# 65 places in the 72-step order of an attention block changed on four engines, and the quantiser's scale computed by GpSimd

## The reference

```python
h = layernorm(x) * (1 + ca) + sa
x = x + ga * attention(h, Wq, Wk, Wv, Wo)     # 32 query heads on 8 key heads of 64, rotary, causal
h = layernorm(x) * (1 + cb) + sb
x = x + gb * ffn(h, w_gate_up, w_proj)
# the ffn's weights are quantised in groups of 64:
#   w = w.astype(bf16); scale = clip(mean(|w|), 1e-8); q = clip(round(w / scale), -1, 1)
#   w + (q * scale - w)
# ffn: silu(gate) * up, rms_norm, projection
```

## Time and profile before

| | us |
|---|---|
| median of 3 runs (lowest, highest) | 1829.48 (1827.33, 1831.39) |
| profiled execution, its own time | 1831.12 |
| its span, first to last instruction | 1829.2 |
| mean granted TensorE clock | 0.990 of full speed |

### The profile page before, as it was taken

The page is one execution under the profiler, slowest core; times in us unless marked ns, Lnnn a source line. Parts: engine busy times, 40 slices in busy tenths (PEclk is TensorE's granted clock), DMA queues, the critical chain, the costliest instruction groups (busy, mean ns, idle before and its releaser), DMA issues. The chain is left out here.

```text
span 1829.2 us, 28097 instructions
## 1 busy us (share of the span) xinstructions
PE 1740.6 (95%) x9505; PEld 1390.7 (76%) x9505; DVE 1249.0 (68%) x2102; ACT 1147.0 (63%) x2315; POOL 968.3 (53%) x773
## 2 busy tenths in 40 slices
PE   7899999999999999999999999988999899999998
PEld 3577777877777777777787787776788788888886
DVE  6788888888787878788888888785333454535343
ACT  4578777777777777877777777795322353323222
POOL 1266757666667676566766666636200044444454
PEclk9899999999999999999999999999999999999999
DMA  7333434344354354344434434455555300101010
GB/s 279 78 103 95 124 103 128 103 108 123 88 132 116 87 129 109 92 120 105 125 104 108 122 89 139 110 162 164 179 180 183 126 1 1 52 1 52 1 30 23
DMA packets 174969, 190.95 MB, mean 104 GB/s; under 512 B 31456, under 2 KB 117736, under 8 KB 174832
## 3 DMA queue, kind: packets, MB, share of 16 engines
q1 hardware_dynamic: 137840, 140.99, 27.1%
q10 hardware_dynamic: 36992, 48.25, 9.5%
HBM read 86.12 MB, written 31.74 MB: 64 GB/s over the span
## 5 line engine op out<-in xcount | busy, mean ns | idle before, releaser
L980 DVE TENSOR_TENSOR p_lo<-ps_b,p_hi 128x512 fp32r<-128x512 f32 x576 | 395.6, 687 | 190.9 <-ACT p_hi L876 187.1
L891 ACT ACTIVATE p<-ps_b,negm 128x640 f32<-128x640 f32 (+7 forms) x512 | 381.8, 749 | 123.2 <-DVE negm L988 120.1
L876 ACT CAST p_hi<-ps_b 128x512 fp32r<-128x512 f32 x576 | 337.2, 588 | 128.1 <-PE ps_b L774 125.5
L988 DVE TENSOR_REDUCE negm<-ps_b 128x1 f32<-128x640 f32 (+7 forms) x512 | 375.7, 744 | 33.3 <-PE ps_b L764 32.5
L774 PE MATMUL ps_b<-ident,p 128*128 128x128 f32 x2304 | 348.7, 274 | 6.2 <-DVE p_lo L980 5.3
L762 PE MATMUL ps_b<-k_hh,q_hl 128*128 128x512 f32 (+3 forms) x768 | 272.7, 355 | 45.5 <-ACT p L891 44.8
L774 PEld LDWEIGHTS ps_b<-ident,p 128*128 128x128 f32 x2304 | 260.3, 141 | 46.7 <-ACT p L891 7.9
L788 PE MATMUL ps_b<-p_hi,v_hl 128*128 128x512 f32 x576 | 269.8, 468 | 5.6 <-ACT o_sb L884 5.2
L763 PE MATMUL ps_b<-k_l,q_hl 128*128 128x512 f32 (+3 forms) x768 | 256.8, 347 | 0.0
L789 PE MATMUL ps_b<-p_lo,v_hl 128*128 128x512 f32 x576 | 227.1, 394 | 0.0
L762 PEld LDWEIGHTS ps_b<-k_hh,q_hl 128*128 128x128 f32 x768 | 145.6, 190 | 94.1 <-ACT p L891 64.8
(11 more groups left out here) (161 smaller groups left out, 3201.8 us busy)
## 6 DMA issues: line engine op xcount, KB each, us to landing
rot_x<-rot_s SPq DMA_DIRECT2D x320, 64.0 KB, 2.0
q_hl<-rot_s SPq DMA_DIRECT2D x128, 128.0 KB, 2.5
q_hl<-rot_x SPq DMA_DIRECT2D x128, 128.0 KB, 2.5
rd_all<-reciprocals SPq DMA_DIRECT2D x128, 128.0 KB, 3.0
o_low<-o_sb ACTq DMA_DIRECT2D x128, 128.0 KB, 2.4
attention_out<-o_sb SPq DMA_DIRECT2D x128, 128.0 KB, 2.5
o_raw<-attention_out SPq DMA_DIRECT2D x32, 512.0 KB, 4.6
wf<-in_L_ffn_w_gate_up ACTq DMA_DIRECT2D x28, 256.0 KB, 3.1
```

The lines of the kernel that those rows point to most:

```text
L876: act.copy(p_hi[:, T % P_RING, :], ps[:, T_BANK + T % 2, :]).then_inc(phi_ready, 1)
L891: act.activation(p_32[:, parity, h, column * P:column * P + nk], s, ACT.Exp, bias=negm[:, k:k + 1], scale=1.0, accum_out=den[:, parity, k: ...
L980: dve.tensor_tensor(p_lo[:, T % P_RING, :], ps[:, T_BANK + T % 2, :], p_hi[:, T % P_RING, :].bitcast(F32), ALU.subtract).then_inc(plo_read ...
L988: dve.tensor_reduce(negm[:, k:k + 1], s, AX.X, ALU.max, negate=True).then_inc(max_ready, 1)
```

## The change

The functions that said in which step a part is due (`rows`, `tile`, `uses`, `pairs`, `units`, `blocks`) are replaced by tables, one for each kind of part, from the part's number to a pair (step, place in the step). Most entries hold the old step and the old order within it. 65 entries are changed ("own" is the old step; a place is a number that sorts the parts within a step). The mask (L764) becomes a part of its own, `masked`, which may stand apart from its row's scores. The scale of a weight unit, 128x8 elements, is computed by GpSimd, in the unit's step 5. `above` is gone: `unit_pick` multiplies by the constant and compares in one scalar_tensor_tensor. `split_weights` is divided in two functions that stand one behind the other in the same step; ScalarE's `unit_parts` is divided likewise.

```diff
+TURNS = Places(own_tiles(0), 100, {
+    11: (10, 303), 19: (18, 511), 20: (19, 511), 25: (24, 511), 35: (34, 511), 39: (38, 301), 66: (65, 101),
+    71: (70, 511)})
+VALUES = Places(own_tiles(LAG), 200, {
+    0: (2, 900), 2: (4, 511), 3: (4, 512), 8: (10, 301), 9: (11, 900), 16: (18, 900), 18: (20, 900), 23: (24, 512),
+    24: (26, 900), 27: (29, 900), 32: (34, 900), 36: (38, 900), 44: (46, 501), 45: (47, 900), 52: (54, 900),
+    54: (56, 900), 55: (58, 101), 60: (62, 900), 63: (65, 900), 68: (70, 900)})
+PROJECTIONS = Places(own_pieces(), 300, {
+    (0, 0): (1, 101), (0, 2): (4, 101), (2, 0): (9, 800), (3, 0): (14, 101), (3, 1): (14, 102), (4, 0): (19, 800),
+    (4, 2): (22, 101), (5, 0): (24, 800), (5, 1): (27, 101), (5, 2): (27, 102), (6, 0): (31, 201), (7, 0): (36, 501),
+    (7, 3): (38, 901), (9, 0): (44, 800), (10, 0): (49, 501), (11, 0): (54, 800), (12, 0): (59, 501), (12, 1): (61, 201),
+    (12, 2): (62, 101), (13, 0): (67, 501), (13, 2): (69, 301)}, early=PROJECTIONS_EARLY)
+VALUE_TURNS = Places(own_uses(("v",), 0), 400, {
+    1: (6, 501), 8: (41, 201)})
+SCORES = Places(own_rows(0), 500, {
+    6: (6, 520), 14: (15, 501), 22: (24, 520), 30: (33, 520), 38: (42, 520), 46: (51, 501), 54: (60, 501), 62: (69, 520)}, early=SCORES_EARLY)
+MASKS = Places(own_rows(0), 510, {
+    6: (6, 530), 8: (10, 302), 14: (15, 530), 22: (24, 530), 30: (33, 530), 38: (42, 530), 46: (51, 530), 54: (60, 530),
+    62: (69, 530)}, early=MASKS_EARLY)
...
+HIGHS = Places(own_tiles(0), 200, {
+    18: (17, 301), 30: (29, 311), 40: (39, 601), 66: (65, 201)})
+SHIFTS = Places(own_blocks(LAG + 1), 310, {
+    13: (67, 401)})
+EXPONENTIALS = Places(own_rows(1), 400, {
+    6: (7, 420), 14: (16, 420), 22: (25, 420), 30: (34, 420), 32: (37, 201), 38: (43, 420), 46: (52, 420), 54: (61, 420),
+    62: (70, 420)}, early=EXPONENTIALS_EARLY)
+KEY_HIGHS = Places(own_uses(("kv",), 8), 500, {
+    13: (76, 201)}, early=in_warm_up(("kv",), KEYS_AT))
+QUERY_HIGHS = Places(own_uses(("qx", "qy"), 8), 510, {
+    4: (28, 101)}, early=in_warm_up(("qy",), QUERIES_AT))
+UNIT_SIGNS = Places(own_units(3), 610, {
+    2: (29, 401), 3: (44, 201)})
+ROTARIES = Places(own_uses(("kv", "qx", "qy"), 4), 100, {
+    7: (38, 301)})
+MAXIMA = Places(own_rows(1), 200, {
+    3: (4, 501), 5: (6, 201), 6: (7, 220), 14: (16, 220), 22: (25, 220), 27: (31, 301), 30: (34, 220), 35: (40, 301),
+    36: (40, 501), 37: (41, 301), 38: (42, 301), 46: (52, 220), 50: (56, 301), 54: (61, 220), 62: (70, 220)}, early=MAXIMA_EARLY)
+RECIPROCALS = Places(own_pairs(0), 400, {
+    7: (66, 301)})
+RECIPROCAL_TURNS = Places(own_pairs(1), 410, {
+    7: (67, 201)})
+UNIT_SUMS = Places(own_units(4), 500, {
+    2: (27, 301), 4: (53, 301)})
+UNIT_PICKS = Places(own_units(7), 510, {
+    0: (8, 301)})
+WEIGHT_LOWS = Places({k: W_LOW + k for k in range(CT)}, 700, {
+    2: (31, 302)})
+HALF_SUMS = Places(own_blocks(LAG + 3), 100, {
+    5: (29, 401)})
+DIVISIONS = Places(own_blocks(LAG + 4), 110, {
+    5: (33, 421)})
+ROTARY_SUMS = Places(own_uses(("kv", "qx", "qy"), 6), 200, {
+    6: (33, 422)})
+UNIT_SCALES = Places(own_units(5), 400)
...
-            def unit_scale(g, u):
-                units_sum.await_(dve, g, u)
-                dve.tensor_scalar(gscale[:], gsum[:], 1.0 / QG, 1e-8, ALU.mult, ALU.max).then_inc(gscale_ready, 1)
-
-            def unit_above(g, u):
+            def unit_pick(g, u):
                 units_scale.await_(dve, g, u)
-                dve.tensor_scalar(above[:], gscale[:], ROUND_HALF, None, ALU.mult).then_inc(above_ready, 1)
-
-            def unit_pick(g, u):
-                units_above.await_(dve, g, u)
                 units_out.await_(dve, g, u - 1)
-                dve.tensor_tensor(w_hat[:].rearrange("p (g e) -> p g e", e=QG), w_abs[:].rearrange("p (g e) -> p g e", e=QG),
-                                  above[:].unsqueeze(2).broadcast_to([P, NG, QG]), ALU.is_gt).then_inc(picked, 1)
+                dve.scalar_tensor_tensor(out=w_hat[:].rearrange("p (g e) -> p g e", e=QG), in0=gscale[:].unsqueeze(2).broadcast_to([P, NG, QG]),
+                                         scalar=ROUND_HALF, in1=w_abs[:].rearrange("p (g e) -> p g e", e=QG), op0=ALU.mult,
+                                         op1=ALU.is_lt).then_inc(picked, 1)
...
+            def unit_scale(g, u):
+                units_sum.await_(pool, g, u)
+                pool.tensor_scalar(gscale[:], gsum[:], 1.0 / QG, 1e-8, ALU.mult, ALU.max).then_inc(gscale_ready, 1)
```

More of the change, by code:

```diff
@@ L356, with __init__, at @@
 CONSTS_AT, KEYS_AT, QUERIES_AT, QUERY_SWAP, TABLE_AT = 60, 12, 12, 59, 53
+USES = {kind: [n for n, x in enumerate(X_USES) if x[0] == kind] for kind in ("kv", "v", "qx", "qy")}
+class Places:
+    def __init__(self, own, place, moved=(), early=()):
+        self.steady, self.early = dict(own), dict(own)
+        self.steady.update(moved)
+        self.early.update(early)
+        for table in (self.steady, self.early):
+            for n, at in table.items():
+                if not isinstance(at, tuple):
+                    table[n] = (at, place)
+        self.slots = set(place for _, place in list(self.steady.values()) + list(self.early.values()))
+        self.found = []
+        for table in (self.early, self.steady):
+            found = {}
+            for n in sorted(table):
+                found.setdefault(table[n], []).append(n)
+            self.found.append(found)
+    def at(self, g, T, place):
+        return self.found[0 if g < 0 else 1].get((T, place), ())
@@ L473, in attention, with __init__, find @@
         class Body:
-            def __init__(self, g, low, high):
-                self.g, self.low, self.high = g, low, high
+            def __init__(self, g):
+                self.g = g
             def holds(self, back, first, last):
-                return first <= self.low - back and self.high - back <= last
-            def rows(self, T, delay):
+                return first <= self.g - back <= last
+            def find(self, T, place, places, ranges):
                 out = []
[L486 to L491, removed]
-                return out
@@ L494, in tile @@
[L494 to L534, removed]
+                for back in (1, 0, -1):
+                    g = self.g - back
+                    for n in places.at(g, T + STEPS * back, place):
+                        first, last = ranges(n)
+                        if first <= g <= last:
+                            out.append((g, n))
@@ L536, in before, with units, halves, bodies @@
+            def units(self, T, place, places):
+                return self.find(T, place, places, lambda u: (0, KVH - 1 if u < LAST_UNITS else KVH - 2))
+            def halves(self, T, place, places):
+                return self.find(T, place, places, lambda n: (0, KVH - 2))
             def before(self, T, at):
                 return T == at and self.g < 0
[L540 to L552, removed]
+        def bodies(step, *tables):
+            slots = sorted({0, SP_REST, ACT_REST, DVE_REST}.union(*[t.slots for t in tables]))
+            steps = ([(Body(-1), T) for T in range(START, STEPS)] + [(Body(g), T) for g in range(KVH) for T in range(STEPS)]
+                     + [(Body(KVH), T) for T in range(14)])
+            for body, T in steps:
+                for place in slots:
+                    step(body, T, place)
@@ L689, in step @@
                         outputs.load_piece(sp, 0, piece)
[L690 to L694, removed]
+                for g, n in body.halves(T, at, WEIGHT_LOADS):
+                    sp.wait_ge(w_ready, CT * (g + 1))
+                    load_weights(sp, wq, wk, wv, w_raw, w_in, g + 1)
+            bodies(step, SWAPS, PLACINGS, SAVES, SPREADS, STORES, WEIGHT_LOADS)
             sp.wait_ge(vectors.gates_out, 16 * 2 * NCH)
@@ L819, in step @@
                         vectors.turn(pe, ps[:, O_BANK, v * CT * B:(v + 1) * CT * B], rd_all[0:B, v, :], ident).then_inc(vectors.late_turned, 1)
-                for g, n, _ in body.uses(T, 0, kinds=("v",)):
-                    await_x(g, n)
[L822 to L831, removed]
+                for g, t in body.whole(T, at, TURNS):
+                    turn(g, t)
+                for g, t in body.whole(T, at, VALUES):
+                    values(g, t)
+                for g, (n, k) in body.pieces(T, at, PROJECTIONS):
+                    project(g, n, k)
+                for g, n in body.uses(T, at, VALUE_TURNS):
+                    await_x(g, n)
                     turn_values(g, n)
-                for g, r in body.rows(T, 0):
+                for g, r in body.rows(T, at, SCORES):
                     scores(g, r)
-                for g, n, k in body.uses(T, 0, kinds=("kv", "qx", "qy")):
-                    project(g, n, 0)
-                for g, t in opens:
-                    values(g, t)
-            bodies(pe, step)
+                for g, r in body.rows(T, at, MASKS):
+                    masked(g, r)
```

(3 more changed lines are left out.)

261 lines of the change are left out of this document (160 added, 101 removed).

## The result

The changed kernel takes 1813.1 us (median of 4 runs, 1810.0 to 1817.0), the kernel before 1830.4 in the same sittings (1827.3 to 1831.7). The ratio is 0.9909, 95% interval 0.9894 to 0.9925: faster by 0.9%. The prediction was 1789 us, a gain of 41 us; the gain is 17. The side is right, the size is less than half.

The account below looks back on a forecast made before the run. TensorE was taken to bound the kernel. Waits 4.4 + switches 1.1 = 5.5 us a body, 7 x 5.5 = 38.5 plus 1.5 in body 7; 1831.1 - 40 = 1791.1, less 1.6 for the median, stated as 1789 us, range 1767 to 1826.

Parts of the forecast that it names:

- What bounds the kernel: One body, 148.4 us: TensorE, busy for 142.8, sets the pace; only its waits and its own instructions' time can shorten it.
- The eight waits and their moves: TensorE's eight waits per body cost 6.8 us; a named move addresses each; 0.65 taken, 4.4 us a body.
- full closing: All eight TensorE waits close and all switches count: 6.8 + 1.4 us a body, 1769 us in all.
- Case D: Rival: everything closes, 7 x (6.8 + 1.4) + 3 = 60 us gained, 1769 us; chance 0.14.
- The fear that VectorE between steps 29 and 33 would take waits back: VectorE there, with two 1.2 us maxima and four weight subtractions, has almost no gaps as the body shrinks.
- Switches: TensorE's changes from masks or transposes to ordinary matmuls: 18 fewer a body at 0.08 us, 1.4; taken as 1.1 us.
- the 8 x 0.17 behind the waits: Each of TensorE's eight waits per body costs 0.17 us more than its shown idle time, making 5.4 us 6.8.
- VectorE's load: Six scales and six `above` leave VectorE's body, 3.9 of 119.7 us; comparisons add 0.3; nothing by itself on TensorE's path.
- The scale on GpSimd: Weight unit's scale on GpSimd: taken as 0.2 us, between 0.16 and 1.14, hidden because VectorE needs it two steps later.
- SyncE and ScalarE queues: Block 5's store delays a swap about 1 us, counted nothing; ScalarE's |w| of unit 3 may wait some 1 us for GpSimd.
- Rival C: GpSimd's lateness reaches TensorE through ScalarE at step 39, costing beyond about 2 us: 25 us slower, 1854; chance 0.11.
- The rule on shared SBUF interfaces: GpSimd contention could hold VectorE's two-input comparison or GpSimd's scale, at 1.14 us; no cost unless GpSimd over 2.5 us late.

Follow-up runs that it names:

- e2: Changed kernel with the product and half sum of output block 5 on GpSimd back in their own steps 29 and 28: 1766.9 us, ratio 0.965.
- e5: Changed kernel with one entry undone, the product of output block 5 on GpSimd back in step 29: 1773.0 us, ratio 0.9697.
- e9: Old order with the quantiser's edit (scale on GpSimd), and only the product of output block 5 moved from step 29 to 33: 1870.3 us, ratio 1.0226.
- e11: Changed kernel with the product of block 5 in step 32, ahead of use 5's query low part, instead of step 33 behind it: 1773.8 us, ratio 0.9698.
- e1: Changed kernel with only the rotary sum of use 6 on GpSimd back in its own step 37 instead of 33: 1799.9 us, ratio 0.983.
- e12: Changed kernel with only the half sum of output block 5 back in step 28, its product still at step 33: 1805.2 us, ratio 0.9877.

## Why the prediction was right or wrong

- **What bounds the kernel: right.** With the waits gone, TensorE is busy for 139.6 of 140.1 us of a body, and the time is 1767.
- **The eight waits and their moves: right, and better than I took them.** I read each wait's closing from the order and then counted 0.65 of it. In e2 all eight are closed: a body goes from 148.4 to about 139.6 us between most of its weight roundings, 8.8 us, where full closing and all switches made 6.8 + 1.4. Case D (1769, chance 0.14) is what this order gives without its two bad entries: 1767, 22 us below the forecast. The two entries then cost 46 us. So the forecast missed by 24 us only because two errors ran against each other. The fear that VectorE between steps 29 and 33 would take waits back was real at one place only, and there by contention.
- **Switches (1.1 us a body): borne out by the rows, timed by no run of their own.** Counted in the traces, ordinary 512-column matmuls behind transposes or a mask are 89 in a body before and 72 in the body of e2, each 0.31 or 0.32 us to the next start against 0.23: 17 x 0.08 = 1.4 us. TensorE's busy time in these bodies falls from 142.8 to 139.6 us, 3.2 us; the 8 x 0.17 behind the waits and the switches make 2.8 of it.
- **VectorE's load (116 us of busy time in a body): missed.** It is 119.5 us in the changed kernel and 119.3 in e2, against 119.7 before, although twelve small instructions are gone. The four weight subtractions of a body take 1.06 and 0.90 us in the mean instead of 0.54, and the new comparison takes 0.80 us in the body of e2 (0.68 in that of the changed kernel; 0.69 before). The two traces do not account for the whole difference; TensorE, which sets the pace, is not late for it in e2.
- **The scale on GpSimd (0.2 us, hidden): right in size,** 0.248 us. It is not wholly hidden, as the prediction had it: VectorE's comparison waits for it ten times, 3.5 us in the whole run. The edit alone moves the time by 3 us.
- **"SyncE and ScalarE queues": the step that failed.** I saw that the product of block 5 would hold up SyncE's store and a swap, priced it at "about 1 us" and wrote "I count nothing for the first". It was 5.6 us of swap and, down the chain, 3.27 us of ScalarE and 3.1 to 3.8 us of TensorE in every body: 40 us in all (e5; 44 by itself, e9). I had taken the product's lateness from its step number, four steps, and had not added the 5.1 us that the low part in front of it waits; ahead of that low part the product costs nothing (e11). Rival C named the place (step 39, unit 2's last operation, tile 40's rounding behind it), the mechanism with its sign, and asked for 2 us of lateness. But it saw the cause in the sum ahead of unit 2, which e1 makes the smaller part, and e9 shows that the chain needs no unit at all.
- **The clock: not in the prediction.** Behind each such wait TensorE also lost about 2.9 us to a granted clock of 0.50. The account: 23.7 us of waits, and (1 - 0.981) x 1810 - (1 - 0.992) x 1770 = 20 us of clock, of which some 7 x 0.5 fall on idle time and are in the waits already: about 41 us together, against 40 measured between the changed kernel and e5.
- **The rule on shared SBUF interfaces (the Trainium skill, GPSIMD Engine Reference, 8. Key points):** I weighed it for the scale and the new comparison only, where it moves nothing on TensorE's path. It acted on an instruction the change does not touch, the second weight subtraction, through a half sum that was moved next to another GpSimd instruction: 6 to 8 us (e5 to e2, the changed kernel to e12). The prediction has no term for the half sum.

## What to carry to other kernels

In a pipeline ordered by hand, price a moved instruction by what it is put behind, not by how many steps it moves, and follow it through every in-order queue that waits for it; a DMA queue is one of them, and what stands behind the store in it is late as well. A wait of some 3 us on TensorE cost nearly double here, because the clock fell with it. When a set of moves gains less than its parts promise, undo the entries of the engine that is not the bottleneck first: here 63 entries and the quantiser's edit gave 3.5%, and two entries took most of it back.

## What the hardware showed that was not expected

- The granted clock fell to 0.50 some 2.6 us into a wait of TensorE of 3.55 us and was 0.50 for over 5 us of the work behind it. In e1 it was 0.50 for about 3.4 us behind a wait of 2.48 us, and its mean is 0.983 against 0.992 in e2. A body of the kernel before, with waits of up to 1.5 us, stayed at 1.00.
- A VectorE subtraction with two SBUF inputs, 0.55 us, took 2.61 us in this body (2.76 at most in the run) when it started within the first of two GpSimd instructions of 1.28 us back to back, and ended 0.4 us after the second. With another pair in e2 it took 1.26 us and ended 0.4 us after the first.
